# Attention over pairs of sequences: nine slots a pair instead of ten, the pairs written out, projection products ahead of head transposes

## The reference

```python
# h: (16, 205, 1024); x = layernorm(h); 32 heads of 32, one shared k and v
qkv = x @ Wqkv                      # 1024 -> 1024 + 32 + 32
scores = einsum('bqhd,bkd->bhqk', q, k) * 32**-0.5
scores = where(causal, scores + slopes * (pos_k - pos_q), -1e30)
attn = einsum('bhqk,bkd->bqhd', softmax(scores), v).reshape(B, S, H)
h = h + attn @ Wo
h = h + ffn(layernorm(h))           # base product, router, 8 low-rank experts
```

## Time and profile before

| what | value |
|---|---|
| median of 3 runs | 1719.29 us (1718.76 to 1721.86) |
| the profiled execution | 1722.0 us, its span 1720.2 us |
| TensorE busy | 1502.7 us, 87% of the span |
| VectorE busy | 1136.6 us, 66% |
| ScalarE busy | 739.5 us, 43% |
| GpSimd busy | 514.4 us, 30% |
| mean granted clock of TensorE | 0.941 |

### The profile page before, as it was taken

The page is one execution under the profiler, slowest core; times in us unless marked ns, Lnnn a source line. Parts: engine busy times, 40 slices in busy tenths (PEclk is TensorE's granted clock), DMA queues, the critical chain, the costliest instruction groups (busy, mean ns, idle before and its releaser), DMA issues. The chain is left out here.

```text
span 1720.2 us, 31628 instructions
## 1 busy us (share of the span) xinstructions
PE 1502.7 (87%) x9700; PEld 1334.9 (78%) x9700; DVE 1136.6 (66%) x4142; ACT 739.5 (43%) x2624; POOL 514.4 (30%) x314
## 2 busy tenths in 40 slices
PE   0254389999999999999999868999999999999999
PEld 0254388787878878887888747999899899998997
DVE  7999277978788787978787856444444454444443
ACT  3355247776777776776787731010111111101100
POOL 1787314354434344444444411001011010010110
PEclk9887689999999999999999669999999999999999
DMA  6134445445454444445464541121121211211211
GB/s 202 37 87 96 104 94 83 98 81 100 74 104 74 109 74 80 98 79 99 79 128 75 123 150 59 54 74 49 61 73 37 73 63 47 73 49 61 74 33 40
DMA packets 110527, 139.63 MB, mean 81 GB/s; under 512 B 13156, under 2 KB 96484, under 8 KB 110040
## 3 DMA queue, kind: packets, MB, share of 16 engines
q1 hardware_dynamic: 110408, 138.41, 35.1%
HBM read 62.82 MB, written 40.30 MB: 60 GB/s over the span
## 5 line engine op out<-in xcount | busy, mean ns | idle before, releaser
L700 ACT ACTIVATE P<-P,nmax 128x128 f32<-128x128 f32 (+1 forms) x1024 | 434.3, 426 | 92.5 <-DVE nmax L790 86.2
L764 POOL TENSOR_TENSOR P<-P,rden 128x512 f32<-128x512 f32 (+1 forms) x256 | 329.2, 1308 | 452.8 <-DVE rden L796 452.6
L790 DVE CUSTOM_DVE_ANT_0 P<-sc,mask 128x128 f32<-128x128 f32 (+1 forms) x1024 | 292.3, 323 | 98.7 <-PE sc L612 92.5
L1129 POOL TENSOR_TENSOR h<-h,base_b 128x1024 f32<-128x1024 f32 (+1 forms) x26 | 62.9, 2418 | 639.2 <-DVE xn L1156 639.2
L802 DVE COPY PTR<-pt 128x282 f32<-128x282 f32 x512 | 222.5, 435 | 35.2 <-PE pt L622 21.3
L642 PE MATMUL pr<-xT_hi,wq_hi 128*128 128x410 f32 x576 | 242.3, 421 | 0.0
L1040 PE MATMUL b<-w_hi,x2T_hi 128*128 128x390 f32 (+3 forms) x624 | 214.7, 344 | 1.0 <-DVE x2T_lo L1166 1.0
L1040 PE MATMUL b<-w_lo,x2T_hi 128*128 128x390 f32 (+3 forms) x624 | 212.9, 341 | 0.0
L1040 PE MATMUL b<-w_hi,x2T_lo 128*128 128x390 f32 (+3 forms) x624 | 212.5, 341 | 0.0
L642 PE MATMUL pr<-xT_lo,wq_hi 128*128 128x410 f32 x576 | 203.4, 353 | 0.0
L642 PE MATMUL pr<-xT_hi,wq_lo 128*128 128x410 f32 x576 | 202.4, 351 | 0.0
(11 more groups left out here) (174 smaller groups left out, 3064.5 us busy)
## 6 DMA issues: line engine op xcount, KB each, us to landing
Qs<-q_hi SPq DMA_DIRECT2D x128, 205.0 KB, 4.7
Qs<-q_lo SPq DMA_DIRECT2D x64, 205.0 KB, 5.5
att_dram<-att SPq DMA_DIRECT2D x64, 205.0 KB, 2.3
at<-att_dram SPq DMA_DIRECT2D x25, 512.0 KB, 4.7
h<-h_dram SPq DMA_DIRECT2D x25, 512.0 KB, 3.3
out<-h SPq DMA_DIRECT2D x25, 512.0 KB, 2.6
h_dram<-Y SPq DMA_DIRECT2D x64, 128.0 KB, 3.1
ht<-h_dram SPq DMA_DIRECT2D x16, 512.0 KB, 5.9
```

The costliest lines, as they stand in the source:

```text
L700: last = nc.scalar.activation(P[rows, j % 2, i, cols], P[rows, j % 2, i, cols], ACT.Exp, scale=-1.0, bias=nmax[at], accum_out=den[at])
L764: lastp = nc.gpsimd.tensor_tensor(w, w, r, ALU.mult)
L790: lastv = v.tensor_tensor_reduce(P[0:n, j % 2, i, cols], sc[i % 2][0:n, cols], mask[0:n, m], 1.0, 3.0e38, ALU.add, ALU.min, nmax[0:n, j % ...
L1129: nc.gpsimd.tensor_tensor(h2[0:n, par, :], h2[0:n, par, :], base_b[0:n, :], ALU.add).then_inc(biased, 1)
```

## The change

The LayerNorm slot is gone. Its transposes are now made in eight chunks of 128 features over all four tiles (`turn_ln`), at the steps `LN_AT` counted from the last slot of the pair before: five chunks in slot 8 beside q7, three in slot 0 beside q0. Six of the chunks use bank 1, two use bank 0; projections alternate between banks 0 and 1, and q7 and the transposes of v use bank 2. ScalarE and VectorE read a chunk one and two steps later (`hi_ln`, `lo_ln`), each with its own counting semaphores. The order of projections is q0, q1, q2, kv, q3 to q7, and units are scored in slots 5 to 8 and 0 to 3 of the next body, without a gap. Pair 0's chunks come in rotation on three banks ahead of its slot 0. All pairs are written out, so the counts are constants. In TensorE's step the projection products and a LayerNorm chunk come ahead of the head's transposes. Statistics and normalisation start two steps later, and SP's loads for the next pair wait for all chunks of this one.

```diff
-SLOTS = 10
+SLOTS = 9
 BANKS = 3
-BANK_USES = 18
...
-    MAIN = ["ln", ("q", 0), ("q", 1), "kv", ("q", 2), ("q", 3), ("q", 4), ("q", 5), ("q", 6), ("q", 7)]
-    USE = {0: 8, 1: 9, 2: 11, 3: 12, 4: 14, 5: 15, 6: 16, 7: 17}
-    KV_USE, VT_USE = 10, 13
+    MAIN = [("q", 0), ("q", 1), ("q", 2), "kv", ("q", 3), ("q", 4), ("q", 5), ("q", 6), ("q", 7)]
+    Q_SLOT = [MAIN.index(("q", k)) for k in range(KC)]
+    KV_SLOT = MAIN.index("kv")
+    MAIN_BANK = [0, 1, 0, 1, 0, 1, 0, 1, 2]
+    VT_BANK = 2
     V_SLOT = 6
-    LN_HI_AFTER, LN_LO_AFTER = 1, 2
-    SCORE_SLOT = [5, 6, 7, 8, 9, 11, 12, 13]
-    def hi_count(use):
-        return use + 1 if use < VT_USE else use
+    LN_SLOT = SLOTS - 1
+    LN_AT, LN_BANK, FIRST_BANK = [0, 1, 3, 4, 6, 8, 10, 12], [0, 1, 0, 1, 1, 1, 1, 1], [i % BANKS for i in range(KC)]
+    def ln_chunk(slot, i, after):
+        at = (slot - LN_SLOT) % SLOTS * GH + i - after
+        return LN_AT.index(at) if at in LN_AT else None
+    def ln_pair(p, slot, first, last):
+        if slot == LN_SLOT:
+            return p + 1 if last is False else None
+        return p if not first and last is not None else None
+    def banks_of(p):
+        return FIRST_BANK if isinstance(p, int) and p == 0 else LN_BANK
+    def last_in(banks, bank):
+        return max(i for i in range(KC) if banks[i] == bank)
+    SCORE_SLOT = [5, 6, 7, 8, 9, 10, 11, 12]
...
-        def run(eng):
-            body(0, True, False)
-            with eng.Fori(1, PAIRS - 1) as p:
-                body(p, False, False)
-            body(PAIRS - 1, False, True)
+        def run():
+            for p in range(PAIRS):
+                body(p, p == 0, p == PAIRS - 1)
             body(PAIRS, False, None)
...
+                    if slot == 1 and last is False:
+                        sp.wait_ge(ln_turned, KC * p + KC)
+                        for s in range(4):
+                            load_h(p + 1, s)
+                    if slot == 1 and last is True:
+                        sp.wait_ge(ln_turned, KC * p + KC)
+                        for k in range(4):
+                            load_wo(k)
...
+            def turn_ln(p, i):
+                banks = banks_of(p)
+                if i == 0:
+                    pe.wait_ge(xn_ready, 4 * p + 4)
+                if banks[i] in banks[:i]:
+                    pe.wait_ge(ln_read, KC * p + max(k for k in range(i) if banks[k] == banks[i]) + 1)
+                else:
+                    wait_count(pe, main_read, SLOTS * p - 2 + banks[i])
+                for s, (c, t0, n) in enumerate(TILES):
+                    at = c * S + t0
+                    last = nc.tensor.transpose(pr[banks[i]][:, at:at + n], ht[0:n, s, i * 128:(i + 1) * 128], ident[0:n, 0:n])
+                last.then_inc(ln_turned, 1)
+            def turn_v(p):
+                wait_apart(pe, main_read, SLOTS * p, const_ready)
+                for c in range(2):
+                    nc.tensor.transpose(pr[VT_BANK][:, 64 * c:64 * c + HD], vT[96:128, c * S:c * S + CH], ident[96:128, 96:128])
+                    last = nc.tensor.transpose(pr[VT_BANK][0:TXT, 64 * c + HD:64 * c + 2 * HD],
+                                               vT[96:128, c * S + CH:(c + 1) * S], ident[96:128, 96:128])
+                last.then_inc(vt_turned, 1)
...
+                    if slot == 0:
+                        pe.wait_ge(ln_read, KC * p + last_in(banks_of(p), 0) + 1)
+                    elif slot == 1:
+                        pe.wait_ge(ln_read, KC * p + KC)
+                    elif slot == SLOTS - 1:
+                        pe.wait_ge(vt_read, p + 1)
+                    else:
+                        pe.wait_ge(main_read, SLOTS * p + slot - 1)
+                if slot == 0 and i > last_in(banks_of(p), 0):
+                    pe.wait_ge(ln_read, KC * p + i + 1)
+                out = pr[MAIN_BANK[slot]][:, 0:PT]
                 if what == "kv":
-                    last = three(pr[use % BANKS][:, 0:PT], wkv, slice(0, 128), i)
+                    last = three(out, wkv, slice(0, 128), i)
                 else:
-                    last = three(pr[use % BANKS][:, 0:PT], wq, slice(128 * what[1], 128 * what[1] + 128), i)
+                    last = three(out, wq, slice(128 * what[1], 128 * what[1] + 128), i)
...
                     for i in range(GH):
                         if sj is not None:
                             scores(*sj, i)
+                        if main is not None:
+                            main_step(p, slot, main, i)
+                        chunk, pair = ln_chunk(slot, i, 0), ln_pair(p, slot, first, last)
+                        if chunk is not None and pair is not None:
+                            turn_ln(pair, chunk)
                         turning = tj if i >= 4 else aj
                         if turning is not None:
                             turn(*turning, (i + 4) % GH)
-                        if main is not None:
-                            main_step(p, slot, main, i)
                         if i == 6 and aj is not None:
                             values(*aj)
             pe.wait_ge(const_ready, 1)
-            visit(body)(pe)
+            for i in range(KC):
+                turn_ln(0, i)
+            visit(body)()
...
+            def hi_ln(p, i):
+                act.wait_ge(ln_turned, KC * p + i + 1)
+                nc.scalar.activation(xT[0][:, i, :], pr[banks_of(p)[i]][:, 0:PT], ACT.Copy).then_inc(ln_hi, 1)
...
-                            hi_part(p - 1, SLOTS - 1, 0)
-                        if i == 0 and slot >= 2 and main is not None:
-                            hi_part(p, slot - 1, 0)
-                        turn = GH * slot + i - LN_HI_AFTER
-                        if 0 <= turn < GH and main is not None:
-                            hi_part(p, 0, turn)
+                            hi_part(p - 1, SLOTS - 1)
+                        if i == 0 and slot >= 1 and main is not None:
+                            hi_part(p, slot - 1)
+                        chunk, pair = ln_chunk(slot, i, 1), ln_pair(p, slot, first, last)
+                        if chunk is not None and pair is not None:
+                            hi_ln(pair, chunk)
...
-        STATS_AT, RSTD_RATE = 12, 1
-        APPLY_AT, APPLY_EVERY = 36, 1
+        STATS_AT, RSTD_RATE = 14, 1
+        APPLY_AT, APPLY_EVERY = 38, 1
...
+            def lo_ln(p, i):
+                dve.wait_ge(ln_hi, KC * p + i + 1)
+                v.tensor_tensor(xT[1][:, i, :], pr[banks_of(p)[i]][:, 0:PT], xT[0][:, i, :].bitcast(F32), ALU.subtract).then_inc(ln_read, 1)
...
+                        chunk, pair = ln_chunk(slot, i, 2), ln_pair(p, slot, first, last)
+                        if chunk is not None and pair is not None:
+                            lo_ln(pair, chunk)
```

More of the change, by code:

```diff
@@ L572, in body @@
                         load_wo(8)
[L573 to L576, removed]
                     if main is not None and slot >= 1 and isinstance(MAIN[slot - 1], tuple):
@@ L580, in body @@
                         stack_q(p - 1, 7)
[L581 to L584, removed]
                     if aj is not None:
@@ L644, in three @@
                 return last
-            def main_step(p, slot, what, i):
[L647 to L658, removed]
+            def turn_ln(p, i):
[10 more added lines that the diff above has]
+                last.then_inc(ln_turned, 1)
@@ L659, in main_step @@
+            def main_step(p, slot, what, i):
                 if i == 0:
                     if slot == V_SLOT:
-                        wait_apart(pe, bank_read, BANK_USES * p + VT_USE - BANKS + 1, const_ready)
-                        for c in range(2):
-                            nc.tensor.transpose(pr[VT_USE % BANKS][:, 64 * c:64 * c + HD], vT[96:128, c * S:c * S + CH], ident[96:128, 96:128])
-                            last = nc.tensor.transpose(pr[VT_USE % BANKS][0:TXT, 64 * c + HD:64 * c + 2 * HD],
-                                                       vT[96:128, c * S + CH:(c + 1) * S], ident[96:128, 96:128])
@@ L667, in main_step @@
-                        last.then_inc(proj_done, 1)
-                    pe.wait_ge(bank_read, BANK_USES * p + use - BANKS + 1)
-                if i == KC // 2 and what == ("q", 0):
-                    pe.wait_ge(bank_read, BANK_USES * p + 8)
+                        turn_v(p)
+                    if slot == 0:
[3 more added lines that the diff above has]
+                    elif slot == SLOTS - 1:
+                        pe.wait_ge(vt_read, p + 1)
+                    else:
+                        pe.wait_ge(main_read, SLOTS * p + slot - 1)
@@ L676, in main_step @@
                 if i == KC - 1:
-                    last.then_inc(proj_done, 1)
+                    last.then_inc(main_done, 1)
             def body(p, first, last):
@@ L749, in _ @@
             act.wait_ge(const_ready, 1)
-            visit(body)(act)
+            for i in range(KC):
+                hi_ln(0, i)
+            visit(body)()
```

(13 more changed lines are left out.)

64 lines of the change are left out of this document (21 added, 43 removed).

## The result

The changed kernel takes 1688.63 us (median of 4 runs, 1687.95 to 1689.26) against 1719.03 us before: a ratio of 0.982 (95% interval 0.9803 to 0.9837), 30.4 us or 1.8% faster. The forecast was 1673 us, 46.8 us faster; the measured time lies inside the range of 1652 to 1700. The direction is right and some 16 us of the saving are missing.

The account below looks back on a forecast made before the run. TensorE, busy 87% of the span, bounds the kernel with holes in four places. Pairs of 84.2 + 3.2 + 1.5 = 88.9 us bring the block from 782.9 to 736.1 us, saving 46.8: 1673 us, range 1652 to 1700.

Parts of the forecast that it names:

- Slots without a hole: TensorE's nine slots of a pair, LayerNorm transposes included, sum to 84.2 us when it waits for nothing.
- VectorE's overhang: Slots 1 to 5: VectorE's statistics, root and normalisation outlast TensorE's work by 3.2 us a pair, bounds 1.7 and 5.5.
- LayerNorm chunks on one bank: Slots 8 and 0: TensorE waits for VectorE to read shared banks, 1.5 us a pair, bounds 0 and 4.6.
- bank chain: Slots 8 and 0: LayerNorm chunks waiting on their bank; slots above 13 us would show the forecast wrong.
- Order within the step: zero: TensorE's step: products ahead of head transposes cost nothing, bounds -0.5 and +1.5 us a pair.
- The tenth slot and the loop's edge: Old LayerNorm slot and return to the loop's top: 4.3 us, five times, and more emptiness go; the edge is 13 us.
- The late stack: Slot 7: TensorE's wait of 2.2 us for q3's stack, six times over the block, goes.
- First pair, pair 7, drain: Block's ends: start 2.5 us later, first pair 59.5 us, pair 7 82.9, drain 57.8, which is 6.6 more.
- C: Rival, chance 0.04: instruction fetch for the written-out pairs makes the kernel 24 us slower, 1743 us.
- A: Rival, chance 0.2: VectorE and ScalarE set the pace of most slots, 92.4 us a pair, 1694 us.
- D: Rival, chance 0.03: the holes only move and TensorE waits elsewhere for the same 11.8 us, 1719 us.

Follow-up runs that it names:

- mixed order: The changed kernel with the head transposes ahead of the projection products in slots 8 and 0 only: 1670.95 us (ratio 0.9715).

## Why the prediction was right in kind and too large

**Slots without a hole (84.2 us): right.** Pair 7's slots 1 to 5 are 45.5, slots 6 and 7 16.7, and slots 8 and 0 are 2 x 9.5 + 8 chunks of 0.36: 84.1 us.

**VectorE's overhang (3.2): right**, 3.6 measured, but with the new order. With the old one, from whose rows it was priced, it is 4.2 (slots 2 to 5 take 10.95, 10.52, 9.09 and 9.59).

**LayerNorm chunks on one bank (1.5): the term that was mis-sized.** 13.23 + 12.33 - 19.0 - 2.9 = 3.7 us a pair. Slot 8, at 13.23, passes the 13 us that the prediction gave as its sign of a bank chain. The mechanism was named, but I let VectorE's copy start when the head transposes of a step ended and did not add that it has to wait for the next step's whole row of products first.

**"Order within the step: zero": the step that failed.** It is the same error in another place. I checked that the head transposes cost TensorE the same wherever they stand, and that two buffers cover the copy, but not what is queued behind the copy on VectorE. The order costs 13.8 us (1688.6 against 1674.8), 2.0 a pair, more than my bound of 1.5: 2.5 lost in slots 8 and 0, some 0.6 gained in slots 2 to 5. With the old order a pair measured 89.5 us, against the 88.9 of the sum: 84.1 + 4.2 of overhang + 1.2 for the chunks, which I had put at 1.5. That the time was then 1674.8, against 1673, is in part luck, by the drain and the start below.

**The tenth slot and the loop's edge: right in sign, and the edge too small.** I priced the edge at 13 us of the saving. In the ten-slot kernel it is 18.8, clock included, in the nine-slot one 31. The sum did not suffer, as it was built from slots that have no edge. The rule of the Trainium skill (Advanced Engine Details and Errata, Control Flow Timing: about 108 ns for a compare-and-branch) does not describe the price of a loop's return here: VectorE's gap is 2.5 to 5.4 us.

**The late stack: right.** No wait of TensorE for `Qs` is left, and none of ScalarE for its q buffers.

**First pair, pair 7, drain.** The start came 0.8 us later than before (2.5 forecast), pair 0 took 60.4 (59.5), pair 7 83.8 (82.9), the drain 54.4 (57.8). That the start and the drain came 1.7 and 3.4 us better than forecast is luck, no term of the sum gave it, and it hides that much of the error in the pairs. All in all the block ends 35.6 us earlier, not 46.8. Behind it the feed-forward block, which I took as unchanged, takes 714.5 us instead of 711.9; its two longest waits for VectorE (`aT_lo` and `h`) grew from 5.6 and 5.2 us to 7.3 and 6.8. The last 2.5 us are the yardstick: the profiled execution of before lay 3 us over its median, that of the changed kernel at 1689.1 only 0.5 over.

**Rivals.** C did not happen: q8 fetched 57 blocks instead of 30, six a pair, and no idle time of TensorE is put down to them; the Trainium skill's rule (same page, ISA Cache) names these fetches rightly, and the trace shows no cost. I looked only at q8. The other queue, q14, fetches more with the loop (89 against 57) and does so where VectorE stands, so the risk that C saw in written-out code may lie in the loop. A's time came near (1694), though not by its cause: slots without statistics or chunks stayed at 9.5 us. With the loop left in, D's number would have come (1719.4), not by its cause: the five returns took 29 us, the rest of a pair was about as short as without the loop.

Left open: whether it is the stack's DMAs that make VectorE's gap at the return longer in the nine-slot loop (3.8 to 5.4 us against 2.5 to 2.7).

## What to carry to other kernels

When an instruction is moved later on one engine, follow not only who waits for it but what stands behind that waiter in its own queue; two buffers for the moved result say nothing of the third tile behind it. An order that helps where the reader engine has too much to do can cost where it has to be prompt, so choose it slot by slot: here the mixed order was 18 us better than the new one and 4 better than the old. Parts of a change need not add: with the old order nine slots were worth some 14 us in a loop and 26 without one. And when an engine stands at a loop's return, look at the instruction queues in the DMA view of that stretch, and at what else the DMA engines move there.

## What was unexpected of the hardware

The return of a hardware loop costs each engine differently and depends on the program: VectorE issued nothing for 2.5 to 2.7 us in the ten-slot loop and for 3.8 to 5.4 in the nine-slot one, ScalarE for 2.3 to 2.9, and TensorE's granted clock over the slot that followed was 0.72 in the ten-slot loop (pair 5) and 0.81 to 0.90 in the nine-slot one, a mix of 2.4 and 1.2 GHz, where it stayed at 1.00 in the same slot written out. Every one of these gaps holds two or three instruction fetches of q14; in the ten-slot loop the DMA engines are busy for some 27% of the gap, in the nine-slot one for all of it.
